# Scaling before transposing at the borders of a blocked triangular solve

## What is computed

```python
logits = jnp.einsum('bhqd,bhkd->bhqk', q, k) * scale
causal_mask = jnp.triu(jnp.full((s, s), -jnp.inf, dtype=logits.dtype), 1)
probs = jax.nn.softmax(logits + causal_mask, axis=-1)
L = jnp.eye(s, dtype=probs.dtype) - jnp.tril(probs, -1)
rhs = jnp.diagonal(probs, axis1=-2, axis2=-1)[..., None] * v
A = jax.scipy.linalg.solve_triangular(L, rhs, lower=True)
```

## Time and profile before

| | |
|---|---|
| median of 3 runs | 1378.62 us (1378.52 to 1380.69) |
| the profiled execution | 1379.12 us, span of its instructions 1377.1 us |
| VectorE busy | 900.3 us, 65% of the span |
| TensorE busy | 969.1 us, 70% |
| ScalarE, GpSimd busy | 464.2 us and 343.4 us |
| row loop, lines 1329 and 1335 | 180.9 and 175.9 us, 992 instructions each |

### The profile page before, as it was taken

One profiled execution on the slowest core, in us unless ns is written; L12 is line 12 of the kernel. 1 busy time (PEld: TensorE's weight loads), 2 busy tenths in 40 slices (PEclk: granted clock), 3 DMA queues, 4 the chain that ended last, 5 costly groups with the idle time before them and its releaser, 6 DMA issues. The chain is left out here.

```text
span 1377.1 us, 29569 instructions
## 1 busy us (share of the span) xinstructions
PE 969.1 (70%) x10741; PEld 766.2 (56%) x10762; DVE 900.3 (65%) x3559; ACT 464.2 (34%) x1066; POOL 343.4 (25%) x390
## 2 busy tenths in 40 slices
PE   5377499990647044976769986869987777987754
PEld 5165399980512023665646565746656665776643
DVE  5656272224779244988768888868878981048967
ACT  2233244434224101421125521135531126941215
POOL 1277155550027262012210012210002130002231
PEclk9997699995569577976779977779986698987777
DMA  9398598846116874510025411033421005421108
GB/s 219 47 204 225 135 253 228 234 133 164 33 34 197 267 179 107 150 42 21 25 70 128 106 44 40 26 96 111 120 67 43 17 29 149 142 57 34 31 30 235
DMA packets 241824, 153.95 MB, mean 112 GB/s; under 512 B 80432, under 2 KB 226096, under 8 KB 241424
## 3 DMA queue, kind: packets, MB, share of 16 engines
q1 hardware_dynamic: 232528, 133.04, 37.6%
q0 software_dynamic: 9152, 19.02, 4.2%
HBM read 96.76 MB, written 55.24 MB: 110 GB/s over the span
## 5 line engine op out<-in xcount | busy, mean ns | idle before, releaser
L1157 DVE TENSOR_REDUCE mx<-banks 128x1 f32<-128x384 f32 (+3 forms) x352 | 203.0, 635 | 67.3 <-PE banks L1088 54.6
L1329 DVE TENSOR_TENSOR prod<-A,Kst_Pn 128x8 f32<-128x8 f32 (+30 forms) x992 | 180.9, 224 | 0.6
L1335 DVE TENSOR_REDUCE A<-prod 128x4 f32<-128x8 f32 (+30 forms) x992 | 175.9, 219 | 0.0
L1137 ACT ACTIVATE Eoff<-banks 128x256 f32<-128x256 f32 (+2 forms) x192 | 114.9, 598 | 101.2 <-PE banks L1073 92.1
L800 POOL DMA_INDIRECT o_dram<-step_o,step_to x80 | 82.5, 1032 | 261.5 <-ACT step_o L789 249.3
L1071 PE MATMUL banks<-Qexp,Kst_Pn 128*128 128x256 bf16 x640 | 115.1, 282 | 36.4 <-DMA Qmax<-q_stack 29.5
L1139 ACT ACTIVATE Ed<-banks 128x256 f32<-128x256 f32 x256 | 98.0, 383 | 110.9 <-PE banks L1073 110.9
L1084 PE MATMUL banks<-masks,identb 128*128 128x128 bf16 (+2 forms) x352 | 89.1, 253 | 61.1 <-DMA Qmax<-q_stack 51.0
L1269 POOL TENSOR_TENSOR A<-A,Kst_Pn 128x256 f32<-128x256 f32 x16 | 19.3, 1205 | 428.1 <-DVE Kst_Pn L1299 428.1
L1088 PE MATMUL banks<-Kst_Pn,Qmax 128*128 128x128 bf16 (+3 forms) x491 | 115.2, 305 | 0.0
L782 ACT ACTIVATE step_h<-banks 128x512 f32<-128x512 f32 x80 | 47.4, 597 | 178.6 <-PE banks L756 178.5
(11 more groups left out here) (197 smaller groups left out, 1808.9 us busy)
## 6 DMA issues: line engine op xcount, KB each, us to landing
Kst_Pn<-k_stack SPq DMA_DIRECT2D x32, 512.0 KB, 4.1
rows_dram<-blank SPq DMA_DIRECT2D x12, 858.0 KB, 12.0
e_w<-in_L_w1T_dram SPq DMA_DIRECT2D x39, 256.0 KB, 2.8
e_w<-in_L_w2T_dram SPq DMA_DIRECT2D x39, 256.0 KB, 3.4
Qmax<-q_stack SPq DMA_DIRECT2D x64, 96.0 KB
Qexp<-q_stack SPq DMA_DIRECT2D x64, 96.0 KB
Kst_Pn<-k_stack SPq DMA_DIRECT2D x16, 384.0 KB, 4.4
step_xt<-rows_dram SPq DMA_DIRECT2D x40, 132.0 KB, 2.2
```

The source lines that it names most:

```text
L1137: nc.scalar.activation(Eoff[:, n % 4, 0:I, :, :].rearrange("p j h q -> p (j h q)"), big[n % n_big][:, 0:I * 2 * P], ACT.Exp, scale=scale)
L1157: nc.vector.tensor_reduce(out, logits, AX_X, ALU.max, negate=True).then_inc(max_done, 1)
L1329: nc.vector.tensor_tensor(prod[:, ds, 0:r + 1], A[:, ds, k0:k0 + r + 1], Pn[:, c * SUB + r:c * SUB + r + 1, 0:r + 1].broadcast_to([P, HD / ...
L1335: nc.vector.tensor_reduce(A[:, ds, k0 + r], prod[:, ds, 0:r + 1], AX_X, ALU.add).then_inc(row_done, 1)
```

## The change

VectorE's order is changed; no instruction is added or removed on any engine. The scaling of the probabilities becomes a function of its own and stands ahead of `keep_rows`. The transposition of the sums and the reciprocal are taken a sub-block ahead: those of sub-block 0 stand before the loop, those of `c + 1` follow the addition in `add_before(c)`.

```diff
-            def add_before(c):
+            def scale_probs(c):
                 for g in range(per_sub * c, per_sub * (c + 1)):
                     gs = slice(g * TURN, (g + 1) * TURN)
                     if g:
@@
                                             ALU.mult).then_inc(probs_in, 1)
+
+            def add_before(c):
                 add_term(c, before[:, :, 0:HD].rearrange("p q d -> p d q"))
+                if c + 1 < NSUB:
+                    turn_before(c + 1)
 
@@
+            turn_before(0)
             for c in range(NSUB):
-                turn_before(c)
+                scale_probs(c)
                 if c:
                     keep_rows(c - 1)
                 add_before(c)
```

## The result

| | before | after |
|---|---|---|
| median | 1379.05 us (10 runs) | 1385.31 us (10 runs) |
| profiled execution | 1379.12 us, span 1377.1 | 1388.69 us, span 1386.8 |
| ratio after / before | | 1.0048, 95% interval 1.0033 to 1.0062 |

The change makes the kernel 6.3 us slower by the medians and 6.6 by the ratio. The profiled execution of the kernel after is the slowest of its ten; it enters the first hop 2.4 us later than the profiled one of before (600.92 against 598.50 in rows 4), ahead of anything that was changed. So I compare hop by hop, from the first transposition to the last copy of solved rows: 112.35, 109.18, 111.87 and 111.86 us before, 113.50, 110.92, 114.28 and 113.19 after. The sum is +6.6 us.

A forecast was written before the change was run, and what follows sets the result against it. The bound was taken as VectorE's row loop, a TensorE-VectorE relay at twelve borders and the serial hop starts. +11.4 - 4.6 = +6.8 us on 1379.12 gives 1385.9, less 0.5 for the median: 1385.4 us, range 1381.5 to 1389.

The forecast's parts named there:

- the borders' gain: At first, second and third borders: copies go sooner once the transposition is out of their way, -4.6 us in sum.
- The exposed transposition: Start of each hop: sub-block 1's transposition and reciprocal add 2.84 us to the path, four times, +11.4 us.
- a fixed rate: Moved transposition at a hop's start: slowed 1.32 times during 2.08 us beside line 1179, so 2.42 us long.
- Bare price: Rival: the moved transposition at a hop's start keeps 1.92 us, so +9.4 - 4.6 = +4.8, 1383.4 us; chance 0.22.
- First borders: First border of each hop: all turns slow, copy at 2.07 us instead of 2.34, 4 x 0.27 = 1.08 us gained.
- Second borders: Second border of each hop: copy sooner by 0.27 three times and 1.0 in the second hop, 1.8 us gained.
- They keep their speeds: TensorE's row turns at second borders: nothing changes ahead of them, so only the second hop's is quick.
- Third borders: Third border of each hop: TensorE comes late from its expert tile; copies gain 0.35 to 0.51, together 1.77 us.
- From copy to addition: Borders: time from the copy's end to the addition stays as now, 5.2 us in the first; another would refute the prediction.
- Waits: VectorE's waiting for line 1228 at the borders, 36.2 us before, becomes about 41 us.
- GpSimd's wait would go: Borders: GpSimd's product ends before VectorE's addition wants it, so that wait, 0.77 us a border, goes; worth nothing.

The follow-up runs named there:

- e2: Kernel before plus one more transposition and reciprocal of sub-block 1 between a hop's first addition and its row loop; 1390.16 us, ratio 1.0071 to before.
- e4: Changed kernel, but TensorE begins line 1179's transposes at a hop's start only after VectorE's transposition of sub-block 1; 1378.33 us, ratio 0.9993 to before.
- e6: Kernel before with the change only at second and third borders, line 1179 delayed, work ahead of a hop's first scaling moved into `attend`; 1367.26 us, ratio 0.9905.
- e5: Kernel before with each border's transposition and reciprocal done twice ahead of the copy; 1405.69 us, ratio 1.0175 to before.
- e7: Kernel before with line 1179's transposes at a hop's start begun only when GpSimd's first product is done; 1379.22 us, ratio 0.9985 to before.

## Why the prediction was right

The forecast was 1385.4 us and the median is 1385.3. That is luck in part: the cost was put 1.1 us too high and the borders' gain 1.5 us too high, and a gain of 0.6 us at the ends of hops was not in the sum. The mechanism, a serial piece at each hop's start against copies that go sooner, is what the runs show.

- **The exposed transposition**, forecast +11.4, is +10.3 in the trace and 9.8 in e2. The step was right, the term too large. I took the slowing from the transposition at the hop's start (1.92 to 2.53) and spread it over 2.08 us of line 1179. The moved one took 2.17, not 2.42. That line 1179 is the cause is shown by e4. That the slowing is a fixed rate was the wrong part. In all 52 cases in the ten traces the transposition ended 0.00 to 0.07 us after the run of line 1179 beside it: at 601.03 against 600.99 in the earlier trace rows, at 609.55 against 609.49 in the kernel after. In e6 one began 0.87 us after the start of a run of 32 transposes (line 1186 there) and took 4.00 us, to 1210.09 against 1210.08:

```profile
1205.22 4.86 PE L1186 MATMUL banks<-ident_c,Ed 32*128 32x32 f32 x32
...
1206.09 4.00 DVE L1178 STREAM_TRANSPOSE before<-RT 128x1024 f32<-128x1024 f32 x1
```

By that reading the moved one ends with line 1179 at 607.05 in the earlier trace rows. From 604.97 that makes 2.5 us with the reciprocal and gaps, 10.0 for four hops. Why it ends there isn't shown. `term` doesn't wait so long: it ended in the middle of line 1179's run, after 0.96 us.

- **Bare price** as a rival: wrong in its reason, 0.25 us off in its number, so that the measured value (2.17) lies halfway between it and the forecast.
- **First borders**: forecast four gains of 0.27, all at 1.2 GHz; measured 0.28, 0.28, 0.27 and 0.28, all at 0.50. In the second hop the turns went from 1.05 to 1.89 us, as foreseen from the longer idle time.
- **Second borders**: forecast 1.8, measured 0.30 + 0.28 + 0.31 + 1.03 = 1.9. But the quick one had moved from the second hop to the fourth. "They keep their speeds" was wrong border by border. In the first and second borders of all ten traces the turns took 1.05 to 1.07 us wherever TensorE's idle time before them was 3.18 us or less, and 1.23 to 1.92 us with 3.29 us or more; the second borders lie on both sides, at 2.7 to 3.9. At hop ends it was not so: 1.09 us after 3.92 to 3.98 us of idle time in e2, e5 and e7, 1.79 after 3.24 in the kernel before. The idle time just before the turns does not settle their speed alone.
- **Third borders**: forecast 1.77, measured 0.41 + 0.45 + 0.42 - 0.17 = 1.1. In the fourth hop TensorE came from its expert tile 1.5 us after the last row instead of 0.8, and the copy then went 2.55 us after it. The kernel before has some of that covered by its own 2.4 us; the kernel after has not.
- **From copy to addition**: the copies gained 4.1 us, the additions of `add_later` 3.1. The products' stops are most of the difference; at the first border of the first hop the one stop took 1.12 to 2.29 us over the ten traces. The prediction had named another time from copy to addition as a sign of being wrong. It is another, 5.40 us instead of 5.24 at that border and 1.0 us more over all twelve; no run separates this from the spread.
- **Ends of hops**: not in the sum. Two of the four last turns were quicker, 0.8 us together, and one, quicker in the kernel before, was slow, 0.2 us. 10.3 - 3.1 - 0.6 = 6.6, the sum measured over the four hops.
- **Waits**: I foresaw 41 us for line 1228 and it is 36.8. The step that failed is that GpSimd's wait would go. It goes at eight borders. At the four third borders it grew, because GpSimd is still sending an expert tile's rows there. VectorE's timeline at the third border of the first hop, the kernel before and then the kernel after:

```profile
684.04 0.43 DVE L1288 TENSOR_TENSOR A<-A,later_term 128x256 f32<-128x256 f32 x1 [0.77 <-POOL A L1269]
```

```profile
687.40 0.43 DVE L1288 TENSOR_TENSOR A<-A,later_term 128x256 f32<-128x256 f32 x1 [1.37 <-POOL A L1269]
```

The wait is 0.77 us before and 1.37 after. It stays beside the products and costs nothing.

## What to carry to other kernels

Work that is moved ahead by one step of a loop lands, in the first step, where there was nothing to hide it: four pieces of 2.6 us in the open cost three times what twelve borders gained. Peel the first step off, or put it under a wait of the stage before. And when work that hid a slower engine is taken from in front of a hand-over, that engine's state begins to count: here the clock that TensorE has after an idle time.

## What the runs showed of the hardware

- TensorE's 32-partition transposes (line 1179) lengthened VectorE's 128x1024 transposition from 1.90 to 2.17 us (to 4.00 in e6) and `term` from 0.57 to 0.96 us. The small reads of the row loop beside them aren't lengthened: the first twelve rows of the first hop take 5.35 us in the kernel before, with 2.08 us of line 1179 beside them, and 5.35 in the kernel after without it.
- GpSimd's product, which the prediction counted among the readers that line 1179 slows, was held up by `term` in the main: 0.85 us where it ran without it, 1.07 to 1.11 behind a `term` of 0.57, 1.53 to 1.57 behind one of 0.94 to 0.96. At the start of the first hop it ended 0.67 us after `term` in e4, without line 1179 beside it, and 0.76 in the kernel after, with it, so line 1179 itself can have cost it 0.1 us. The reverse happens too. At the first border of e4's third hop the product and the sending of an expert tile's rows (line 800) run in front of and beside `term`, which took 1.75 us:

```profile
1053.91 0.96 POOL L800 DMA_INDIRECT o_dram<-step_o,step_to  x1 [0.30 <-issue]
1054.39 1.75 DVE L1287 TENSOR_TENSOR later_term<-before,rZ 128x256 f32<-128x256 f32 x1
...
1054.89 0.87 POOL L1271 TENSOR_TENSOR A<-A,Kst_Pn 128x256 f32<-128x256 f32 x1
```

That looks like one instruction holding the other off for its whole length. "SBUF — State Buffer" of the Trainium skill (section "SBUF: two separate sides") states it so for a GpSimd instruction and a VectorE one with two inputs in that memory, as `term` has. These rows agree; no run here was made for it.
